# Key tiles in groups of three, three and two, and v's first half ahead of the keys, in a two-layer graph network

## The reference

```
A    = |  |sigmoid(c_adj_j - c_adj_i) - 0.5| - 0.5 | * 2        # c_adj: mean of x over channels
g    = relu((x^T @ (adj * A_s)) * para)                        # 256 x 1024 per batch; gives q
k, v = split(x @ kv_w)                                         # 4 heads of 64 channels
out  = softmax(q k^T * scale) v
x1   = layernorm(x + out)
```

## Time and profile before

| | us |
|---|---|
| timed runs, median (lowest to highest) | 2866.09 (2864.56 to 2866.31) |
| the profiled execution: its time | 2866.0 |
| the profiled execution: its span | 2864.0 |

### The profile page before, as it was taken

The page is one execution under the profiler, slowest core; times in us unless marked ns, Lnnn a source line. Parts: engine busy times, 40 slices in busy tenths (PEclk is TensorE's granted clock), DMA queues, the critical chain, the costliest instruction groups (busy, mean ns, idle before and its releaser), DMA issues. The chain is left out here.

```text
span 2864.0 us, 39358 instructions
## 1 busy us (share of the span) xinstructions
PE 2711.2 (95%) x12436; PEld 1850.8 (65%) x12436; DVE 1988.9 (69%) x2859; ACT 1663.1 (58%) x2146; POOL 1279.5 (45%) x684
## 2 busy tenths in 40 slices
PE   7999999999999999999999999996799999989964
PEld 5565665656656566665656656563688888878854
DVE  6687786877878687786877878784633333348878
ACT  6566576766667666576666767653422222237768
POOL 3755647565474755657566474745200000000025
PEclk9999999999999999999999999998899999999976
DMA  4123222232222232222232222220332223305556
GB/s 136 60 84 101 74 66 84 63 106 84 66 73 77 73 97 86 73 66 85 64 105 86 65 72 77 84 71 30 120 104 88 88 94 107 108 16 190 190 229 256
DMA packets 126943, 272.01 MB, mean 95 GB/s; under 512 B 11952, under 2 KB 62128, under 8 KB 123312
## 3 DMA queue, kind: packets, MB, share of 16 engines
q1 hardware_dynamic: 126896, 271.42, 29.4%
HBM read 178.79 MB, written 62.98 MB: 84 GB/s over the span
## 5 line engine op out<-in xcount | busy, mean ns | idle before, releaser
L303 POOL TENSOR_TENSOR psum<-psum,probs 128x1024 f32<-128x1024 f32 x320 | 784.3, 2451 | 144.2 <-ACT probs L373 118.1
L373 ACT ACTIVATE probs<-sc_ps 128x1024 f32<-128x1024 f32 x512 | 508.0, 1024 | 410.4 <-PE sc_ps L822 328.9
L552 DVE TENSOR_REDUCE mx<-mx_ps 128x1 f32<-128x512 f32 x768 | 520.2, 690 | 275.3 <-PE mx_ps L791 273.5
L838 PE MATMUL pv_ps<-probs,v 128*64 128x512 f32 x2048 | 492.4, 604 | 0.0
L822 PE MATMUL sc_ps<-qa,ka 128*128 128x512 f32 x1024 | 387.4, 404 | 0.0
L822 PE MATMUL sc_ps<-qb,kb 128*128 128x512 f32 x1024 | 380.6, 394 | 0.5
L791 PE MATMUL mx_ps<-ka,qa 128*128 128x512 f32 x768 | 315.4, 424 | 10.2 <-DVE mx L552 2.9
L838 PEld LDWEIGHTS pv_ps<-probs,v 128*64 128x64 f32 x2048 | 125.6, 136 | 224.5 <-issue 193.6
L822 PEld LDWEIGHTS sc_ps<-qa,ka 128*128 128x128 f32 x1024 | 187.5, 188 | 106.2 <-issue 64.1
L791 PEld LDWEIGHTS mx_ps<-ka,qa 128*128 128x128 f32 x768 | 139.8, 187 | 179.6 <-issue 77.9
L1177 DVE TENSOR_TENSOR agg_lo<-ag_ps,agg_hi 128x1024 fp32r<-128x1024 f32 x32 | 39.2, 1225 | 310.7 <-ACT agg_hi L1104 310.7
(11 more groups left out here) (195 smaller groups left out, 5548.2 us busy)
## 6 DMA issues: line engine op xcount, KB each, us to landing
adj_ring<-in_adj_dram SPq DMA_DIRECT2D x128, 512.0 KB, 3.7
pre_scratch<-pre SPq DMA_DIRECT2D x28, 1024.0 KB, 4.4
pre<-pre_scratch SPq DMA_DIRECT2D x28, 1024.0 KB, 4.9
x<-in_x_dram SPq DMA_DIRECT2D x16, 1024.0 KB, 5.6
kb<-ka SPq DMA_DIRECT2D x64, 256.0 KB, 3.1
res<-in_x_dram SPq DMA_DIRECT2D x16, 1024.0 KB, 5.6
x_scratch<-res SPq DMA_DIRECT2D x16, 1024.0 KB, 4.5
x1s<-x_scratch SPq DMA_DIRECT2D x16, 1024.0 KB, 7.5
```

The lines of the kernel that those rows point to most:

```text
L303: pool.tensor_tensor(psum[:, h % 2, :], probs[:, 0, :] if k == 1 else psum[:, h % 2, :], probs[:, k % PR, :], ALU.add).then_inc(s["pool_ad ...
L373: nc.scalar.activation(probs[:, i % PR, :], sc_ps[:, t % 2, :], ACT.Exp, scale=SCALE)\
L552: nc.vector.tensor_reduce(mx2[:, nh, n:n + 1], mx_ps[:, nh, :], AX.X, ALU.max)\
L838: ins = nc.tensor.matmul(pv_ps[nh * HD:(nh + 1) * HD, h % 2, :], v[:, i, h * HD:(h + 1) * HD], probs[:, i % PR, nh * BANK:(nh + 1) * BANK] ...
```

## The change

The tiles go in groups 0 to 2, 3 to 5 and 6 to 7; the values of a group follow its own scores at once. `sum_up` moves behind the values of group 0, `transpose_sums`, `transpose_maxima` and `transpose_back` stay behind the scores of group 1 and 2. `MAX_HALVES` has 5, 7 and 4 halves per group (head 0's: 4, 8 and 4). ScalarE's `prepare` goes by tile: in head 3 `xt_high` and `w_high` stand after the exponentials 2 and 5 (before: 1 and 3), the rest after exponential 7 (before: 5). In the bubble, v's first half goes ahead of the keys on TensorE, and `v_copy(b, 0)` ahead of `k_high` on ScalarE; a third tile of `x_high` comes behind `v_copy(b, 1)`. On VectorE `weigh(b, 7)` goes ahead of `add_head(b - 1, 3)`.

```diff
-    MAX_HALVES = [[[0, 2, 1], [2, 1, 1, 1, 0], [2, 1, 1, 1, 1], [1, 1, 0, 0, 0]]] + \
-        2 * [[[0, 1, 1, 1, 1], [1, 1, 1, 1, 0], [2, 1, 1, 1, 1], [1, 1, 0, 0, 0]]]
+    MAX_HALVES = [[[0, 1, 1, 1, 1], [2, 1, 1, 1, 1, 1, 1], [2, 1, 1, 0, 0]]] + \
+        2 * [[[0, 1, 1, 1, 1, 1, 0], [2, 1, 1, 1, 1, 1, 0], [2, 1, 1, 0, 0]]]
+    GROUPS = [range(0, 3), range(3, 6), range(6, 8)]
...
+            def prepare(b, h, i):
+                if h == 2 and i in (3, 5, 7):
+                    distance(b, i // 2 - 1)
+                    tanh_half(b, i // 2 - 1)
+                if h == 3 and i in (2, 5):
+                    xt_high(b, i // 3)
+                    w_high(b, i // 3)
+                if (h, i) == (3, 7):
                     w_high(b, 2)
...
                 q_high(b, 3)
-                k_high(b, 2)
-                k_high(b, 3)
+                v_copy(b, 0)
                 relu_q(b, 1)
...
+                k_high(b, 2)
+                k_high(b, 3)
                 if not last:
-                    x_high(b + 1, range(2, 6))
+                    x_high(b + 1, range(2, 5))
                 v_copy(b, 1)
                 if not last:
-                    x_high(b + 1, range(6, T))
+                    x_high(b + 1, range(5, T))
                 for h in range(HEADS):
+                    for i in range(T):
+                        exponential(b, h, i)
+                        if before and h == 0 and i in (1, 3):
+                            normalise(b - 1, range(2 * i - 2, 2 * i + 2))
+                        if h and i == 1:
+                            head_copy(b, h - 1)
+                        if h and i == 3:
+                            den_copy(b, h - 1)
                         if not last:
+                            prepare(b + 1, h, i)
...
                 w_low(b, 5)
+                weigh(b, 7)
                 if before:
                     add_head(b - 1, HEADS - 1)
-                weigh(b, 7)
...
                 g_product(b)
-                k_piece(b, 0, 0)
-                k_piece(b, 0, 1)
+                v_product(b, 0, [0, 1])
                 max_scores(b, 0, 0)
                 max_scores(b, 0, 1)
+                for n in (2, 3):
+                    v_product(b, 0, [n])
+                    max_scores(b, 0, n)
+                for n in range(4):
+                    k_piece(b, n // 2, n % 2)
+                    max_scores(b, 0, 4 + n)
                 v_product(b, 1, [0, 1])
                 transpose_maxima(b, 0)
...
+                    for g, group in enumerate(GROUPS):
+                        units = [(n, (0, 1), [nh]) for n in group for nh in range(NH)]
+                        if g == 0:
+                            units[0:2 * NH] = [(n, [part], range(NH)) for part in range(0 if h else 1, 2) for n in (0, 1)]
                         for k, (n, parts, part_halves) in enumerate(units):
+                            maxes(g, k)
                             scores(b, h, n, parts, part_halves)
+                        maxes(g, len(units))
...
+                        if h and g == 2:
                             transpose_back(b, h - 1)
+                        if h == 3 and not last:
+                            if g < 2:
+                                transpose_x(b + 1, g)
+                            else:
+                                k_product(b + 1)
+                        for i in group:
+                            values(b, h, i)
+                        if h and g == 0:
                             sum_up(b, h - 1)
```

More of the change, by code:

```diff
@@ L63, in attention_layer @@
     WR, DR, AR, PR = 3, 3, 2, 4
-    PAIRS = T // 2
     SG = P // 4
@@ L67, in attention_layer @@
     SQ = SN // P
-    MAX_HALVES = [[[0, 2, 1], [2, 1, 1, 1, 0], [2, 1, 1, 1, 1], [1, 1, 0, 0, 0]]] + \
-        2 * [[[0, 1, 1, 1, 1], [1, 1, 1, 1, 0], [2, 1, 1, 1, 1], [1, 1, 0, 0, 0]]]
-    SUM_PAIR, DEN_PAIR, BACK_PAIR = 1, 2, 3
+    MAX_HALVES = [[[0, 1, 1, 1, 1], [2, 1, 1, 1, 1, 1, 1], [2, 1, 1, 0, 0]]] + \
+        2 * [[[0, 1, 1, 1, 1, 1, 0], [2, 1, 1, 1, 1, 1, 0], [2, 1, 1, 0, 0]]]
+    GROUPS = [range(0, 3), range(3, 6), range(6, 8)]
     POOL_ADDS = T - 2
@@ L452, in body @@
                     x_high(b + 1, range(0, 2))
-                v_copy(b, 0)
+                k_high(b, 2)
+                k_high(b, 3)
                 if not last:
-                    x_high(b + 1, range(2, 6))
+                    x_high(b + 1, range(2, 5))
                 v_copy(b, 1)
                 if not last:
-                    x_high(b + 1, range(6, T))
+                    x_high(b + 1, range(5, T))
                 for h in range(HEADS):
[L460 to L464, removed]
-                        if not last:
[L466 to L470, removed]
+                    for i in range(T):
[6 more added lines that the diff above has]
+                            den_copy(b, h - 1)
+                        if not last:
+                            prepare(b + 1, h, i)
             x_high(0, range(T))
@@ L898, in body, with maxes @@
                     halves = iter(range(NH * T))
-                    def maxes(p, k):
-                        for j in itertools.islice(halves, MAX_HALVES[h][p][k] if more else 0):
+                    def maxes(g, k):
+                        for j in itertools.islice(halves, MAX_HALVES[h][g][k] if more else 0):
                             max_scores(b, h + 1, j // NH, [j % NH])
[L904 to L910, removed]
+                    for g, group in enumerate(GROUPS):
+                        units = [(n, (0, 1), [nh]) for n in group for nh in range(NH)]
+                        if g == 0:
+                            units[0:2 * NH] = [(n, [part], range(NH)) for part in range(0 if h else 1, 2) for n in (0, 1)]
@@ L911, in body @@
                         for k, (n, parts, part_halves) in enumerate(units):
-                            maxes(p, k)
+                            maxes(g, k)
                             scores(b, h, n, parts, part_halves)
-                        maxes(p, len(units))
-                        if h and p == DEN_PAIR:
+                        maxes(g, len(units))
+                        if h and g == 1:
                             transpose_sums(b, h - 1)
-                        if more and p == PAIRS - 1:
+                        if more and g == 2:
@@ L918, in body @@
                             transpose_maxima(b, h + 1)
-                        if h and p == BACK_PAIR:
+                        if h and g == 2:
                             transpose_back(b, h - 1)
-                        if not last:
-                            prepare(b + 1, h, p)
-                        if h and p == SUM_PAIR:
-                            sum_up(b, h - 1)
[L925 to L930, removed]
@@ L931, in body @@
-                values(b, HEADS - 1, T - 2)
-                values(b, HEADS - 1, T - 1)
+                        if h == 3 and not last:
[6 more added lines that the diff above has]
+                        if h and g == 0:
+                            sum_up(b, h - 1)
             pe.wait_ge(s["ident_set"], 3)
```

## The result

| | us |
|---|---|
| before, median of 4 runs (lowest to highest) | 2866.20 (2864.56 to 2867.61) |
| after, median of 4 runs (lowest to highest) | 2994.86 (2992.50 to 2995.42) |
| ratio, 95% interval | 1.0446 (1.0433 to 1.0459) |
| span of the profiled execution after | 2992.8 |

The account below looks back on a forecast made before the run. The prediction took TensorE's queue, busy 95% of the span, plus its waits to bound the kernel. Its eight terms summed to +142.5 us on 2866.0, giving 3009 us, with a range of 2945 to 3060.

Parts of the forecast that it names:

- term 1: TensorE's blocks of values: 12 a batch instead of 15 save edge costs, -17 us.
- term 2: Bubble: with v's first half ahead of the keys, v's second half no longer waits for its buffer, -12.5 us.
- Term 3: Head 0's maxima: three halves no longer stand in a row, each has two score matmuls beside it, -18 us.
- term 4: VectorE's `weigh(7)` ahead of `add_head`: `w_low(6)` comes 0.74 us later and TensorE waits for it, +11 us.
- term 5: A group's third tile waits for the first one's exponential, and in heads 1 and 2 for VectorE's reductions, +70 us.
- Term 8: Head 3: `transpose_back` waits for the reciprocal behind VectorE's queue, which takes turns with GpSimd, +43 us.
- rival A: In head 3 `weigh(2)` misses its turn and two GpSimd adds go first: +35, 3044 us, chance 0.18.
- rival B: In head 3 VectorE's chain isn't held up by GpSimd's adds: 41 us less, 2968 us, chance 0.13.
- Term 6: Heads 0 and 2: values wait for their own group's exponentials where ScalarE has other work between, +31 us.
- term 7: Maxima: two halves at once at a group's start and the last merge make TensorE wait for VectorE, +35 us.
- Rival C: Within groups TensorE doesn't wait, as exponentials and reductions come back in time: 2830 us, chance 0.04.

Follow-up runs that it names:

- b_block: The kernel before with the values of pair 2 torn in two in each head, 64 blocks of values more in all: 2888.9 us.
- a_weigh: The changed kernel with `add_head(b - 1, 3)` ahead of `weigh(b, 7)` again in VectorE's queue: 2983.1 us.
- a_add: The changed kernel with `add_last(b, h - 1)` ahead of the reductions of the first tile of maxima in heads 1 and 2: 2982.2 us.
- a_half: The changed kernel with each exponential as two instructions of 512 columns, the first already freeing half of its score buffer: 3020.3 us.
- b_best: The kernel before with the change's bubble and head 0's halves of maxima reordered so that no three stand in a row: 2860.5 us.
- a_inv: The changed kernel with `invert_sums(b, 2)` ahead of `xt_low(b + 1, 1)` instead of behind `w_low(b + 1, 1)` in VectorE's queue: 2969.2 us.
- b_bubble: The kernel before with the change's bubble alone (v's first half, `v_copy(b, 0)`, `x_high` in lots of 2, 3 and 3): 2859.5 us.
- a_act: The changed kernel with ScalarE's side work (normalise, distance, tanh) moved behind the last exponential of a group: 2981.2 us.
- a_pairs: The changed kernel with groups of two tiles, each with its own values at once, and the maxima's halves as in the kernel before: 3083.6 us.

## Why the prediction was right

The direction and the range held and the time was 14 us high (3009 for 2994.9, a change of 142.5 for 128.7).

- **Terms 1 to 5 and 8** hold within 0.25 us a batch each, by the table. 1 and 4 were shown alone (b_block, a_weigh), 5's reductions by a_add (head 2) and its exponentials by how the steps moved in a_half; no run takes the exponentials' part away without a side effect (none has a third buffer for the scores), so the 4.3 us are read from the steps, not from a difference of times. Term 3's saving is real in this order of the work, but b_best shows that it isn't there for the taking.
- **Term 8**: the mechanism and its turn-taking held, so rivals A and B fell. One sentence was wrong: "VectorE's preparation gets ahead meanwhile, which gives nothing back". It does give back: a_inv gained only 26 us of the 47, as `add_last(3)` had been hidden behind this very wait. Net of that, the term alone is worth about 1.4 us less a batch than its wait is long.
- **Term 6 was mis-sized**: +2.1 forecast, 1.1 measured. I strung together whole durations. ScalarE starts the next instruction some 0.1 us before the record of the last ends: in head 0 the normalisation starts at 1114.33, 0.90 behind the second exponential's start, and the third exponential 1.97 behind that, where I had taken 1.02 and 2.07:

```profile
1112.52 1.93 ACT L372 ACTIVATE probs<-sc_ps 128x1024 f32<-128x1024 f32 x2
1114.33 2.07 ACT L392 ACTIVATE res<-res,shift,rstd 128x256 f32<-128x256 f32 x4
1116.30 1.01 ACT L372 ACTIVATE probs<-sc_ps 128x1024 f32<-128x1024 f32 x1
```

  Three such overlaps are 0.3 us, and the first wait shrank from 0.7 to 0.41 by just that. I had counted TensorE by starts and ScalarE by durations. That is 15 us too much; term 7 has 6 too much and the other terms together some 7. The other way, some 7 us (0.4 a batch) stand in no term, and the slow steps below add 8. So errors of 28 us and of 15 us the other way leave 14: that the total comes so near is in part luck.
- **Term 7**: 2.15 forecast, 1.75 measured; the merge with the reciprocal in between waits 0.23 us in heads 1 and 2 as in head 0, not 0.4.
- **Not foreseen**: slow steps in five batches (below), some 8 us the other way. The prediction put the clock at nothing, without a word on it.
- Rival C, that nothing waits in a group, fell with the first step of 0.66.

## What to carry to other kernels

Before tiles are regrouped to save edges between blocks of values, count the buffers between producer and consumer: with two, the third tile of a group stands behind a full matmul, read-out and release of the first, and that costs more than the edges saved (4.3 us against 1.0 here). When one queue's step moves later, follow the whole queue behind it on the next engine to whoever waits there, since work of another stage may lie in between. And after a wait is taken away, look where the next one in line was hidden: two removals here (a_inv, b_bubble) gave about half until a second move followed.

## What the runs showed of the hardware

**TensorE's clock after a short stop.** In the trace after, `k_product` runs behind the wait of 2.85 us between starts. In ten batches its steps are 0.23 us; in the other five, 5 to 8 of the 12 are slow, 0.43 us; in the batch shown those from the fifth on. TensorE in such a batch:

```profile
1327.46 0.66 PE L859 MATMUL pv_ps<-ident,heads_t 128*128 128x128 f32 x4 [2.46 <-DVE rden L570]
...
1328.42 0.40 PE L683 MATMUL mx_ps<-xT_lo,kvw_hi 128*128 128x512 f32 x1
1328.66 0.45 PE L683 MATMUL mx_ps<-xT_hi,kvw_hi 128*128 128x512 f32 x1
1328.90 0.63 PE L683 MATMUL mx_ps<-xT_hi,kvw_lo 128*128 128x512 f32 x1
1329.33 0.63 PE L683 MATMUL mx_ps<-xT_lo,kvw_hi 128*128 128x512 f32 x1
```

Busy times by window, after (us; then PE, PEld, DVE, ACT, POOL with their counts, granted clock, DMA share, GB/s), a usual batch first and then windows of the slow one:

```profile
1194.00:1199.00 5.00, 2.54 (x14) 1.83 (x13) 5.00 (x3) 4.89 (x5) 4.84 (x2) 1.00 0.00 0
1326.00:1331.00 5.00, 3.54 (x13) 2.90 (x14) 5.00 (x4) 3.19 (x4) 3.38 (x2) 0.78 0.00 0
1331.00:1334.00 3.00, 3.00 (x12) 1.15 (x10) 1.21 (x2) 1.48 (x2) 0.00 (x0) 0.79 0.00 0
```

A step of 0.427 against 0.227 us for 512 columns is the lower level, 1.2 GHz: where all steps are slow, in a_half from 1209.66 to 1216.00, the granted clock is 0.53. Values of 0.78 and 0.79 are means over a part of the window at 1.2 GHz and the rest at 2.4. It costs 1.6 us in such a batch. With the wait gone no step is slow (a_inv, where the longest one left in these stages is 1.73 us), so the wait brings it. But the wait's length alone doesn't say whether: steps of 2.85 us at `transpose_back` have slow ones behind them in 5 of 15 batches here, in 3 in a_weigh, 4 in a_add and 10 in a_act, and steps of 2.85 us at `transpose_x` in all 15 in a_pairs; 3.29 us (a_half) bring it in 14 of 15, with more slow steps. What else decides stays open. The Trainium skill ("TensorE: Matmul & The Clock Gate", Part 1: The HAM clock gate) has the same two levels.

**VectorE and GpSimd take turns.** Where both have instructions with two SBUF operands ready, VectorE's ends 1.08 to 1.09 us behind the end of GpSimd's add, in the four places shown (two in the earlier trace rows, two above). So a VectorE instruction of 1.2 us costs 1.5 to 3.4 us by where its request falls in the other's, and GpSimd's add, 2.38 us alone, takes 3.15. The time shows as a longer record and not as idle time.
